# Two fused transformer layers on one Trainium2 core: the fp4 rounding steps of h moved one or two quads later in the second layer's schedule

## The reference

```
x = x + causal attention (16 heads of 8)                         first layer
x = x + mixture of 8 experts, the 2 best, 128 -> 512 -> 128      first layer
x = x + attention without a mask (16 heads of 8)                 second layer
x = x + fp4_linear(silu(fp4_linear(x, w_gate)) * fp4_linear(x, w_up), w_down)     128 -> 352 -> 128

fp4_quant_dequant, over blocks of 16 along the last dimension:
    scale = max(max(|x|) / 6, 1e-12);  q = (nearest of 0, .5, 1, 1.5, 2, 3, 4, 6 to |x / scale|) * sign * scale
```

## Time and profile before

| what | value |
|---|---|
| median of 3 runs | 2206.26 us (2202.10 to 2206.92) |
| the profiled execution | 2203.53 us, of which the span from the first to the last instruction is 2201.8 us |
| granted TensorE clock | 0.961 over the span |
| busy, of the span | PE 1959.7 us (89%), DVE 1631.8 (74%), ACT 1428.1 (65%), POOL 1127.5 (51%) |
| the row maxima on DVE, L2370 | 512 of mean 1217 ns, 597.1 us |
| the second layer's quads | 1113.7 to 2117 us; from batch 5 on the row maxima of a batch start 64.7 us behind those of the one before, but once 66.3 (batch 12) |
| chain that ended last | PE 24% of the span, DVE 16%, issue 4%, ACT 2%, POOL 1%; its costliest line is L2370 on DVE, 9% |

### The profile page before, as it was taken

How to read it: one execution, slowest core, us unless ns; L and a number is a source line. 1 busy time by engine, 2 the same in 40 slices (tenths; PEclk the granted TensorE clock), 3 DMA queues, 4 the chain that set the end, 5 groups by cost and what they waited for, 6 DMA issues and landing times. The chain is left out here.

```text
span 2201.8 us, 48376 instructions
## 1 busy us (share of the span) xinstructions
PE 1959.7 (89%) x13892; PEld 998.6 (45%) x14051; DVE 1631.8 (74%) x4372; ACT 1428.1 (65%) x3354; POOL 1127.5 (51%) x1882
## 2 busy tenths in 40 slices
PE   5999999999999957999969888899988889898985
PEld 1455555555555537999922223333333333333333
DVE  7888888887888734443367788888888887888855
ACT  0666766666676644555537777777777777777774
POOL 6334746546474263344345465656665665664221
PEclk7999999999999978999979999999999999999998
DMA  3342323222232122222322212122222212211100
GB/s 97 86 137 73 95 78 94 83 83 86 83 91 81 42 81 71 71 75 84 95 67 66 64 59 66 58 64 63 63 63 66 65 56 63 65 57 54 57 6 15
DMA packets 144100, 155.34 MB, mean 71 GB/s; under 512 B 32160, under 2 KB 111712, under 8 KB 143584
## 3 DMA queue, kind: packets, MB, share of 16 engines
q1 hardware_dynamic: 131888, 131.84, 20.0%
q0 software_dynamic: 8192, 16.79, 2.7%
q10 hardware_dynamic: 3760, 3.62, 0.6%
HBM read 102.87 MB, written 47.71 MB: 68 GB/s over the span
## 5 line engine op out<-in xcount | busy, mean ns | idle before, releaser
L2370 DVE TENSOR_REDUCE l_rowmax<-pair 128x2 f32<-128x1024 f32 x512 | 597.1, 1217 | 134.1 <-PE pair L2046 134.1
L2245 ACT ACTIVATE l_probs<-bank 128x512 f32<-128x512 f32 x1024 | 554.9, 602 | 86.1 <-PE bank L2057 60.7
L1008 DVE CUSTOM_DVE_ANT_0 pair<-pair,mask_rows_q 128x512 f32<-128x512 f32 (+3 forms) x1024 | 476.7, 519 | 80.0 <-PE pair L718 72.9
L887 ACT ACTIVATE l_probs<-bank 128x256 f32<-128x256 f32 (+3 forms) x769 | 307.9, 444 | 106.9 <-PE bank L732 102.7
L718 PE MATMUL pair<-k_stack,q_stack 96*128 96x512 bf16 (+3 forms) x1024 | 316.0, 313 | 22.0 <-DVE l_rowmax L1008 13.5
L2057 PE MATMUL bank<-q_stack,k_stack 128*128 128x512 bf16 x929 | 298.5, 387 | 28.8 <-ACT l_probs L2245 13.6
L2069 PE MATMUL bank<-l_probs,v_aug 128*32 128x512 f32 x2048 | 278.3, 615 | 4.4 <-ACT l_oT L2302 2.6
L2046 PE MATMUL pair<-k_stack,q_stack 64*128 64x512 bf16 x1024 | 178.3, 394 | 79.5 <-DVE l_rowmax L2370 70.1
L730 PE MATMUL bank<-q_stack,k_stack 128*128 128x384 bf16 (+3 forms) x720 | 212.9, 299 | 0.2
L744 PE MATMUL bank<-l_probs,v_aug 128*32 128x512 f32 (+3 forms) x2048 | 191.9, 447 | 20.5 <-ACT l_probs L887 18.1
L2057 PEld LDWEIGHTS bank<-q_stack,k_stack 128*128 128x128 bf16 x1024 | 74.9, 97 | 248.2 <-ACT l_probs L2245 138.1
(11 more groups left out here) (359 smaller groups left out, 3408.2 us busy)
## 6 DMA issues: line engine op xcount, KB each, us to landing
q_stack<-scratch SPq DMA_DIRECT2D x192, 96.0 KB
k_stack<-scratch SPq DMA_DIRECT2D x180, 96.0 KB
q_stack<-scratch SPq DMA_DIRECT2D x320, 48.0 KB
k_stack<-scratch SPq DMA_DIRECT2D x300, 48.0 KB
scratch<-l_q_parts SPq DMA_DIRECT2D x31, 384.0 KB, 2.5
scratch<-l_k_parts SPq DMA_DIRECT2D x30, 384.0 KB, 2.6
experts_rows<-rows_in SPq DMA_DIRECT2D x136, 64.0 KB, 1.8
rows_out<-experts_y SPq DMA_DIRECT2D x68, 128.0 KB, 1.8
```

The lines of the kernel that those rows point to most:

```text
L887: nc.scalar.activation(probs[:, (a * HG + j) % PSLOTS, c0:S], bank[:, c0:S], ACT.Exp, scale=SCALE).then_inc(t_read, 1)
L1008: nc.vector.tensor_tensor_reduce(scores, scores, m["mask_rows_q"][:, S - keys(t):S], 1.0, LOWEST, ALU.add, ALU.max, rowmax[:, g % 2, c:c + ...
L2245: nc.scalar.activation(probs[:, (a * HG + j) % PSLOTS, :], bank[:, :], ACT.Exp, scale=SCALE).then_inc(t_read, 1)
L2370: nc.vector.tensor_reduce(largest, banks[:, :].rearrange("p (k n) -> p k n", k=2), X_AXIS, ALU.max).then_inc(s_read, 1)
```

## The change

Six entries of the tables change, all for the batches 0 to 13 and all of the quantiser of h. No instruction is added or taken away, and the last two batches keep their tables.

| step | engine | place before | place after |
|---|---|---|---|
| `hscales` | POOL | 12 | 13 |
| `hinverse` | DVE | 12, with `stats` | 13 |
| `hquotient` | DVE | 13 | 14 |
| `hsizes` | ACT | 14 | 15 |
| `hraised` | DVE | 15 | 1 |
| `hlowered` | DVE | 0, with `stats4` | 2 |
| `hq` | POOL | 1 | 3, behind two of `gather` |

```diff
-        ("normalise4", 0, F + 24, EARLY), ("xsizes", 0, F + 27, EARLY), ("hsizes", 0, F + 36, EARLY),
+        ("normalise4", 0, F + 24, EARLY), ("xsizes", 0, F + 27, EARLY), ("hsizes", 0, F + 37, EARLY),
...
-                ("hinverse", 0, F + 34, EARLY), ("hquotient", 0, F + 35, EARLY), ("hraised", 0, F + 37, EARLY),
-                ("hlowered", 0, F + 38, EARLY)]
+                ("hinverse", 0, F + 35, EARLY), ("hquotient", 0, F + 36, EARLY), ("hraised", 0, F + 39, EARLY),
+                ("hlowered", 0, F + 40, EARLY)]
...
-    POOL_WORK += [("xscales", 0, F + 26, EARLY), ("xq", 0, F + 30, EARLY), ("hscales", 0, F + 34, EARLY), ("hq", 0, F + 39, EARLY),
+    POOL_WORK += [("xscales", 0, F + 26, EARLY), ("xq", 0, F + 30, EARLY), ("hscales", 0, F + 35, EARLY), ("hq", 0, F + 41, EARLY),
```

## The result

| | before | after |
|---|---|---|
| median | 2202.99 us (5 runs beside the changed kernel) | 2227.69 us (5 runs, 2226.97 to 2231.27) |
| ratio, 95% interval | | 1.0108, 1.0090 to 1.0125 |
| profiled execution | 2203.53 us, span 2201.8 | 2231.27 us, span 2229.5 |
| granted TensorE clock | 0.961 | 0.953 |
| quads of the second layer, first to last start of the maxima | 1113.7 to 2115.9 us | 1117.7 to 2142.8 us |

The change makes the kernel 1.1% slower, 25 us. The forecast was 2202.6 with a range up to 2209, so it was wrong, and slower was the side to which it gave the smallest chance, 0.11. Between the first and the last quad the profiled execution lost 22.9 us (1025.1 instead of 1002.2) and behind the last quad 0.8.

The account below looks back on a forecast made before the run. No engine is full; PE's and DVE's timelines decide. Eleven periods gain 0.2 us each (2.2), two more gain 2.3 together, the last loses 0.8: -3.7 us, so 2202.6 us as median, range 2191 to 2209.

Parts of the forecast that it names:

- What bounds the kernel: One period of 64.7 us: neither DVE (busy 53.9) nor PE (58.4) bounds it throughout, so the engines' timelines decide.
- the count to place 3: DVE's step sum from place 12: place 1 starts 2.8 us earlier, place 3 at 1746.5 instead of 1747.18.
- lead of 2.4 us: PE in place 15: `down` starts at 1731.43 instead of 1733.84; 1.3 us of this is left at `probs_v`.
- wait for ACT: PE in place 0 waits before its last score, as `hsizes` precedes the exponentials in ACT's queue; named as 1.3 us.
- The first gather: POOL beside `hlowered`: held up, it takes about 2.5 us instead of 1.11, and `hq` runs from 1751.4 to 1754.0.
- The port doesn't bite: Rival, chance 0.24: the first gather gets by, `hq` comes 1.4 us sooner, eleven periods keep 1.1 us each; 2192.6 us.
- Place 3 takes 3.15: DVE's place 3 takes 3.15 us and place 4 3.82, place 5 starting 1.15 us sooner if nothing collides.
- POOL keeps the port: Rival, chance 0.11: POOL's next instruction goes before the waiting DVE quotients of h and x; 0.9 us a period, 2213 us.
- two periods without gathers: `hq` can run at 1746.6 and is done by 1749.3, so each keeps the whole 1.15 us; 2.3 us together.

## Why the prediction was wrong

- *What bounds the kernel, and the count to place 3*: right. Place 1 was forecast 18.8 us behind place 12, and it started 18.77 behind (1760.83 to 1742.06). PE's `probs_v` of place 0 started 15.38 us behind place 12, and 16.67 before (from 1720.22), so of its lead of 2.4 us 1.3 were left, as reckoned. Its wait for ACT is there, 0.88 us. The prediction named 1.3 for it, which in its own sum is the lead that is left; the wait of that sum is about 1.1:

```profile
1757.12 0.39 PE L2057 MATMUL bank<-q_stack,k_stack 128*128 128x512 bf16 x1 [0.88 <-ACT l_probs L2245]
```

  The quotient of h took 1.91 us (1.86 forecast), and `factors4`'s sixth piece took 1.51 (its neighbours 0.20).
- *"The first gather"*: wrong. It started 24.8 us behind place 12, as reckoned, and within 0.01 us of `hlowered`. But it took its usual 1.11 and `hlowered` took 0.05 more. I had carried the 1.50 of the earlier trace rows over from a multiply (TENSOR_TENSOR), behind which the gather began 0.08 us, to the rounding (SCALAR_TENSOR_TENSOR), with which it began level; which of the two differences let it pass wasn't tested. So `hq` came 1.4 us sooner than in the sum, as the rival *The port doesn't bite* had it. The Trainium skill (SBUF — State Buffer, "Who interferes with whom") infers that a two-input DVE instruction doesn't hold up a gather; this row agrees. The gather of 1.50 us in the earlier trace rows and one of 1.29 beside the quotient of x in the kernel with gathers later (1682.26) don't.
- *"Place 3 takes 3.15"*: this is the step that failed. It took the divisor of x along at its 0.18, with no collision. I had asked of the two-input instructions alone what POOL runs beside them. The divisor met `hq`, took 3.10 us in each of eleven periods, 2.92 more, and place 3 lasted 6.0 us instead of 3.15. The Trainium skill (the same page and section) lists `tensor_scalar` among the operations that can enter the modes that take the shared port pair. The trace agrees beside `hq` (2.40 beside it alone, 3.11 beside a gather and it), and that sentence should have put L156 on the list. Beside a gather alone the divisor took 0.44 in some periods and 0.18 in others.
- *"POOL keeps the port"* was the right mechanism, with a chance of 0.11, at the wrong instruction: it was priced for the two quotients at 0.9 us a period and gave 2213. Its argument against itself, that DVE came next in the collisions shown, rested on POOL's gap of 0.08 us there. Here the gap is 0.03 and POOL wins, eleven times in eleven. The kernel with `hq` at place 4, with a gap of 0.07, is no contest: its next maxima had started before the gather ended. Between the earlier trace rows and the changed kernel the instructions differ as well as the gap (a quotient behind a normalise there, a divisor behind a gather here), so that the gap decides is not shown.
- *The size.* The collision costs 2.92 and without it a period gains 1.25, so it should lose 1.67. Three periods of the changed kernel, against 64.70 in the steady part of the kernel before:

```profile
1607.12:1675.36 68.24, 61.91 (x349) 21.57 (x348) 56.31 (x72) 48.68 (x95) 39.10 (x59) 0.95 0.20 60
1675.36:1742.06 66.70, 60.39 (x349) 21.58 (x348) 56.31 (x72) 48.61 (x95) 39.10 (x59) 0.97 0.21 61
...
1809.06:1875.47 66.41, 59.48 (x349) 21.21 (x348) 56.10 (x72) 48.74 (x95) 39.09 (x59) 1.00 0.21 61
```

  The two periods with the whole clock lose 1.71 and 1.73 us; the five with 0.97 lose 2.0 to 2.5 (the first of them 1.2), and the four with 0.95 lose 3.4 to 3.5. Eleven times 1.72 is 18.9; two periods at the end, with no slow divisor, gave 1.2 and 0.2 back (the prediction had 1.15 for each of two periods without gathers), so 17.5 of the 22.9 us are the collision less the gain. The other 5.4 are the difference of two things: the nine periods with less than the whole clock lose 8.5 us beyond 1.72 each, and the kernel before has 3.2 of its own, mostly its two jumps of 1.57. The kernels of the first and fourth session that avoid the slow divisor have a clock of 1.00 over the whole stretch from 1346 to 1860 us; the changed kernel has 0.96. So the fall goes with PE's wait of about 3.0 us, but the wait isn't enough: it stands in all eleven periods, and in two of them the clock stays whole. In the period of 66.41 us, with a clock of 1.00 throughout:

```profile
1842.78 0.63 PE L2103 MATMUL pair<-ident,l_oT 128*128 128x128 f32 x4 [3.02 <-DVE l_rowmax L2370]
```

  That the wait brings the fall about, where it comes, was argued from the order in time and not tested by itself.

## What to carry to other kernels

When a long POOL instruction moves, list every DVE instruction that may meet it, the tiny ones as well: a divisor of 0.18 us, started beside a POOL instruction that ends with another one ready, waited for both here, and everything behind it on DVE waited too. A step sum can be right to 0.1 us up to place 3 and lose its sign in the next place, so the last question about a moved instruction is what runs beside it at its new place. And before a chain's slack is spent, move the other side of the collision (the gathers, `hq`, the divisor): three small edits of the schedule each turned +1.1% into -0.6 to -0.8%.

## What the runs showed of the hardware that was not expected

- A DVE instruction that has started beside one POOL instruction isn't safe from the next. With at most 0.03 us between a gather and `hq` the divisor ended behind `hq` (3.10 us for an instruction of 0.18), in 22 of 22 periods of two kernels.
- An indirect DMA on POOL can stretch a tensor-scalar of 128x32 on DVE to the gather's end (0.44 instead of 0.18, in 22 of 43 periods), but the next DVE instruction starts 0.09 us behind its start all the same. A gather that begins level with a 128x1408 scalar-tensor-tensor takes its usual 1.11, and that one 0.05 more.
- DVE's reciprocal (L162) took its usual 0.34 us beside `hq`.
- The same kernel took 2204 us in two sessions and 2282 in two others. The one trace of it at 2282 has nearly the same starts up to place 4 of each period and losses of 1 to 3 us in single places from there on, whose cause is open. One version gained 1.0% in one session and lost 0.5% in another, so both have to be run before an order of work is kept.
